# Four runs of unit-matrix products on TensorE, put into four of its pauses in a small vision tower

## The chip, the cores and the metric

The program runs on one core of a Trainium2 chip. The core's engines are TensorE (PE in the profile; PEld is its weight load, PEq or PEldq its instruction queue), VectorE (DVE), ScalarE (ACT), GpSimd (POOL) and SyncE (SP, which here only issues transfers). The metric is the device time of one execution in microseconds, the median of several runs.

## The reference

Inputs are 128 images. A token stage cuts each into 81 patches (a 14x14 convolution to 256 channels), attends over 3x3 windows and adds a class token, which gives h of 128 x 10 x 256. Four residual layers follow, each behind a layer norm:

```
h = tok(x, ...)                              # convolution, window attention, class token
h = h + attention0(layernorm(h), ...)        # 16 heads, 10 tokens, biases
h = h + moe(layernorm(h), ...)               # 8 experts, top 2, gelu, layer norm per expert
h = h + attention1(layernorm(h), ...)        # causal, scores clipped
h = h + lowrank(layernorm(h), ...)           # base matrix, shared and 6 routed low-rank pairs
```

The router picks two of eight experts for each of the 1280 tokens:

```
logits = x_flat @ router_w
gate_vals, gate_idx = jax.lax.top_k(logits, TOP_K)
h = jax.nn.gelu(jnp.einsum('nd,edf->enf', x_flat, w1) + b1[:, None, :], approximate=False)
out = jnp.einsum('enf,efd->end', h, w2) + b2[:, None, :]
```

## The kernel before

Each engine has its instructions written out by hand in one block, in the order in which it runs them, and semaphores tie the engines together. A matmul on fp32 operands shows as two MATMUL records (and two weight loads) in the profile; one on fp32r or bf16 operands, or a transpose, shows as one.

The stages in order of the span, with what TensorE does in them:

- **Convolution and window attention, from 13 to some 372 us.** TensorE waits for `consts_made` and `wc_made`, then for the first patch's operands (`x_lo_made`), and runs `LEAD` = 11 convolutions and then nine rounds.
- **Attention 0, to some 461 us.** Queries, keys and values, score sums with the unit matrix, output projection, and the router's logits.
- **Routing, to 482 us.** `pe_experts` begins with two products that count tokens per expert (lines 1682 and 1683, semaphore `route_summed`). VectorE (`dve_route`) works out each pair's place from them and writes one-hot matrices in four groups of five pairs (`row_hot_made`, line 1906). TensorE multiplies them (line 1689, `pairs_done`), VectorE turns the sums into tables of row numbers, GpSimd gathers the rows with indirect transfers (`rows_loaded`), and `turn_rows(0)` transposes the first 128 rows.
- **Experts, 482 to 681 us.** 27 blocks of 128 rows. For each, eight times `up` (line 1708, two 128x128 fp32 products) and `down` (line 1716, one 128x256 fp32 product), with gelu on ScalarE between them; `down` runs three behind `up`. Then gates are transposed, the experts' beta is added with eight-row products (line 1739), and two products with `z_w` (line 1744, semaphore `z_summed`) prepare the last layer.
- **Barrier, then the combine, attention 1 and the low-rank layer, 692 us to the end.** SyncE reads the experts' results back (`yl`), VectorE adds them to h and takes statistics (`dve_combine`), and attention 1 starts when its first tiles are normalized.

Between the experts and the combine stands a barrier over all five engines, `phase(eng, 2)`; the same call with 1 stands between the token stage and attention 0. Its two lines are

```
eng.drain().then_inc(sem("phase_ended"), 1)
eng.wait_ge(sem("phase_ended"), 5 * n)
```

so each engine goes on when all five have drained, and the drain is line 286 in the profile. On TensorE the order at that place is `pe_experts(pe)`, `phase(pe, 2)`, `pe_attention(pe, 1)`; on SyncE it is `phase(sp, 2)`, `sp_combine(sp)`.

The matmul destinations are PSUM banks 0 to 7; `bank(i, a, b)` is columns a to b of bank i. `ident` is the 128x128 fp32 unit matrix, one of the constants behind `consts_made`.

Of the kernel before, what the change touches and what calls it, by code (L numbers as in the profile page):

```python
# [22 lines left out]
P = 128  # L23
# [46 lines left out]
def vision_tower(nc, d, out):  # L70
    ctx = ExitStack()
    with ctx:
        def sb(name, shape, dt=F32, scope=None):
            return (scope or ctx).enter_context(nc.sbuf_tensor(name, shape, dt))
# [3 lines left out]
        def sem(name):  # L78
            if name not in sems:
                sems[name] = ctx.enter_context(nc.semaphore(name))  # L80
            return sems[name]
# [4 lines left out]
        def bank(i, a=0, b=C):  # L86
            return pair[i // 2][:, i % 2, a:b]
# [3 lines left out]
        ident = sb("ident", [P, P])  # L91
# [60 lines left out]
        rows = sb("rows", [P, len(ROWS) * C], F32, tok)  # L152
# [53 lines left out]
        count = sb("count", [P, P], F32, route)  # L206
# [94 lines left out]
        def turn(pe, dst, src):  # L301

            for c in range(CH):
                last = pe.transpose(dst[:, c * P:(c + 1) * P], src[:, c * P:(c + 1) * P], ident[:, :])  # L304
            return last

        class Chain:

# [105 lines left out]
        def conv(pe, i):  # L414
            k = i % RING_X
            if i >= 2:
                pe.wait_ge(sem("summed"), i - 1)
            pe.wait_ge(sem("x_lo_made"), 2 * i + 2)
            if i == NP:
                pe.wait_ge(sem("wc_made"), 7)  # L420
            for c in range(KF):
                a = [x[:, k, c * P:(c + 1) * P] for x in (x_hi, x_lo)]
                mm3(pe, bank(i % 2), a, (wc_hi[:, c, :], wc_lo[:, c, :]), c == 0, False)
            fourth, fifth = [x_hi[:, k, c * P:(c + 1) * P] for c in (KF, KF + 1)]
            if i < NP:
                last = mm3(pe, bank(i % 2), (fourth, fifth), (tail_hi, tail_lo), False, True)
            else:
                pe.matmul(bank(i % 2), fourth, wc_hi[:, KF, :], start=False, stop=False)
                last = pe.matmul(bank(i % 2), fifth, wc_hi[:, KF + 1, :], start=False, stop=True)  # L429
            last.then_inc(sem("conv_done"), 1)  # L430
# [58 lines left out]
        def turn_patch(pe, j):  # L489
            pe.wait_ge(sem("xn_made"), j + 1)  # L490
            if j >= 2:
                pe.wait_ge(sem("xg_lo_made"), j - 1)
            turn(pe, bank(2 + j % 2), xn[:, j % RING_XN, :]).then_inc(sem("xT_done"), 1)
# [1174 lines left out]
        def down_bank(s):  # L1668
            return bank(2 + 2 * (s % 2))

        def weights_of(s):
            r = s % RING
            return (w1raw[r], w2raw[r]) if r < 2 else (w1more[r - 2], w2more[r - 2])

        def loads_before(s):

            return s // RING

        def pe_experts(pe):
            pe.wait_ge(sem("route_consts"), ROUTE_CONSTS)  # L1680
            pe.wait_ge(sem("route_ready"), CH + 1)
            pe.matmul(bank(5, 0, E), before[:, :], rank[:, :, T - 1], start=True, stop=True)
            pe.matmul(bank(5, E, 2 * E), ones[:, :], rank[:, :, T - 1], start=True, stop=True)\
              .then_inc(sem("route_summed"), 1)

            for q in range(NPAIR):
                pe.wait_ge(sem("row_hot_made"), q // 5 + 1)
                pe.wait_ge(sem("col_hot_made"), 2)
                last = pe.matmul(bank(7, 0, 2 * NS), row_hot[:, q, :], col_hot[:, q, :], start=(q == 0), stop=(q == NPAIR - 1))
            last.then_inc(sem("pairs_done"), 1)  # L1690

            def turn_rows(s):
                pe.wait_ge(sem(f"rows_loaded{s % AHEAD}"), 16 * (s // AHEAD + 1))
                if s >= 2:
                    pe.wait_ge(sem("xT_made"), s - 1)
                elif s == 1:
                    pe.wait_ge(sem("tables_made"), 2)
                turn(pe, bank(6 + s % 2), xg[:, s % AHEAD, :]).then_inc(sem("rows_turned"), 1)

            def up(s, fc):  # L1700
                if fc == 0:
                    pe.wait_ge(sem("xT_made"), s + 1)
                    pe.wait_ge(sem(f"w_loaded{s % RING}"), 32 * (loads_before(s) + 1))
                g = s * FC + fc
                if g >= 2:
                    pe.wait_ge(sem("gelu_made"), g - 1)
                for c in range(CH):
                    last = pe.matmul(bank(fc % 2, 0, P), weights_of(s)[0][:, c * FF + fc * P:c * FF + (fc + 1) * P],  # L1708
                                     xT[:, s % 2, c * P:(c + 1) * P], start=(c == 0), stop=(c == CH - 1))
                last.then_inc(sem("up_done"), 1)  # L1710

            def down(s, fc):
                pe.wait_ge(sem("gelu_made"), s * FC + fc + 1)
                if fc == 0 and s >= 2:
                    pe.wait_ge(sem("res_made"), s - 1)
                last = pe.matmul(down_bank(s), hid[:, s % 2, fc, :], weights_of(s)[1][:, fc * C:(fc + 1) * C],  # L1716
                                 start=(fc == 0), stop=(fc == FC - 1))
                if fc == FC - 1:
                    last.then_inc(sem("down_done"), 1)

            turn_rows(0)
            for g in range(NS * FC + LAG):
                if g < NS * FC:
                    up(*divmod(g, FC))
                if g >= LAG:
                    down(*divmod(g - LAG, FC))
                if g < NS * FC and g % FC == 2 and g // FC + 1 < NS:
                    turn_rows(g // FC + 1)

            pe.wait_ge(sem("gates_made"), 1)  # L1730
            for i, (a, b) in enumerate(GROUPS):
                for t in range(a, b):
                    last = pe.transpose(bank((0, 1, 3)[i], (t - a) * P, (t - a + 1) * P)[0:E, :], gates[:, t, :], ident[:, :])
                last.then_inc(sem("g_turned"), 1)
            for t in range(T):
                pe.wait_ge(sem("gT_made"), t // 4 + 1)
                if t >= 4 and t % 2 == 0:
                    pe.wait_ge(sem("beta_added"), t // 2 - 1)
                last = pe.matmul(bank(6 + t // 2 % 2, t % 2 * C, (t % 2 + 1) * C), gT[:, t, :], beta[:, :], start=True, stop=True)
                if t % 2:  # L1740
                    last.then_inc(sem("beta_done"), 1)
            pe.wait_ge(sem("z_loaded"), 64)
            for c in range(CH):
                last = pe.matmul(bank(5, 0, ZW + C), ones[:, :], z_w[:, c, :], start=(c == 0), stop=(c == CH - 1))
            last.then_inc(sem("z_summed"), 1)

        def load_weights(sp, s, e):
            if s >= RING:
                sp.wait_ge(sem("down_done"), s - RING + 1)
            for dst, name in zip(weights_of(s), ("w1", "w2")):  # L1750
                sp.dma_start(dst[:, :], d[name][bass.ds(e * P, P), :]).then_inc(sem(f"w_loaded{s % RING}"), 16)
# [457 lines left out]
        @block.tensor  # L2209
        def _(pe):  # L2210
            pe.wait_ge(sem("consts_made"), 4)
            pe.wait_ge(sem("wc_made"), 4)
            for i in range(LEAD):
                if i == LEAD - 1:
                    turn_patch(pe, 0)
                conv(pe, i)
                if i == 1:
                    pe.wait_ge(sem("bias_columns"), CH)
                    mm_rows(pe, bank(4, 0, 2 * C), aggT, wkv_raw, 0, 2 * C).then_inc(sem("kvb_done"), 1)
                if i == 4:  # L2220
                    pe.wait_ge(sem("kvb_made"), 1)
                    turn(pe, bank(6), kvb[:, C:2 * C]).then_inc(sem("kvb_done"), 1)
                if i == LEAD - 1:
                    pe.wait_ge(sem("tok_w_loaded"), 128)
                    pe.wait_ge(sem("kvbT_made"), 1)
                    mm_rows(pe, bank(7), redT, w_proj, 0, C).then_inc(sem("kvb_done"), 1)
            pe.wait_ge(sem("wkv_lo_made"), CH)
            for n in range(NW):
                round_pe(pe, n)
            pe_end(pe)  # L2230
            phase(pe, 1)
            pe_attention(pe, 0)
            pe_experts(pe)
            phase(pe, 2)
            pe_attention(pe, 1)
            pe_lora(pe)
# [146 lines left out]
```

## Time and profile before

| | us |
|---|---|
| median of 3 runs | 802.9 (801.75 to 803.13) |
| the profiled execution, its own time | 801.32 |
| span of the profiled execution, first to last instruction | 799.3 |
| TensorE busy | 708.0 (89% of the span) |
| VectorE, ScalarE, GpSimd busy | 514.5, 378.1, 424.9 |
| TensorE's mean granted clock | 0.942 of 2.4 GHz |

The own time of the profiled execution is 2.0 us over its span, and 1.6 us under the median of the three. A busy TensorE says only that matmuls were under way, since they are pipelined and their ends are modelled. The granted clock of a stretch is 1.00 (2.4 GHz) or 0.50 (1.2 GHz); a mean between the two is a stretch that has both. The profile shows 1.00 from the start of the span until the first change of level that it recorded, whatever the engine ran at; in that stretch the spacing of the matmuls tells the level.

### The profile page before, as it was taken

The numbers are of one execution on the slowest core, as the hardware profiler recorded it, in microseconds if no ns is written. First come the engines' busy times: TensorE is split into PE (matmuls) and PEld (weight loads), VectorE is DVE, ScalarE is ACT, GpSimd is POOL, SyncE is SP. The second block draws the span as 40 slices with busy tenths as digits, with TensorE's granted clock in tenths as the row PEclk, the third lists the DMA queues.
The fourth block names the chain that finished last, engine by engine and source line by source line (L and its number), as shares of the span: only waits on it lengthen the run. The fifth ranks groups of instructions, "written<-read, shape, count | busy, mean of one in ns | idle before, by whom it ended". The sixth has DMA issues, their size and how long they took to land.

```text
span 799.3 us, 13085 instructions
## 1 busy us (share of the span) xinstructions
PE 708.0 (89%) x4247; PEld 606.5 (76%) x4247; DVE 514.5 (64%) x1230; ACT 378.1 (47%) x930; POOL 424.9 (53%) x360
## 2 busy tenths in 40 slices
PE   3879999999999999999829828999999999587797
PEld 2869998988889897654528727999999999344786
DVE  5758787878778777769989871322332223488957
ACT  4466666657666665533132323444444444056131
POOL 5765767677685771448959512333433332036640
PEclk9989999999999999999868967999999999689799
DMA  7952343333423220000020078899988982300001
GB/s 234 257 168 75 114 115 94 84 109 115 113 61 114 58 81 26 1 0 1 0 106 1 27 281 302 309 326 329 327 323 328 347 314 75 129 16 2 0 1 66
DMA packets 47065, 108.58 MB, mean 136 GB/s; under 512 B 5029, under 2 KB 24729, under 8 KB 39577
## 3 DMA queue, kind: packets, MB, share of 16 engines
q1 hardware_dynamic: 44408, 100.68, 37.7%
q0 software_dynamic: 2592, 7.10, 2.4%
q8 instruction: 35, 0.57, 0.3%
q14 instruction: 30, 0.24, 0.1%
HBM read 101.58 MB, written 6.17 MB: 135 GB/s over the span
## 4 chain that ended last, share of the span: by engine, by line
PE 74%; DVE 12%; DMA 4%; SPq 3%; POOL 3%; ACT 2%; issue 2%; DVEq 0%; ACTq 0%; POOLq 0%
PE banks L1708 12%; PE banks L1716 12%; PE banks L291 9%; PE banks L293 9%; PE banks L292 8%; PE banks L298 6%; PE banks L304 4%; PE banks L1316 3%; SPq L386 2%; DMA xraw<-in_x_rest 2%; PE banks L1363 1%; DVE banks L1490 1%; PE banks L1290 1%; DVE a_o L1581 1%; DVE a_prod L1203 1%
## 5 line engine op out<-in xcount | busy, mean ns | idle before, releaser
L408 POOL TENSOR_TENSOR x_lo<-xraw,x_hi 128x512 fp32r<-128x512 f32 x81 | 106.1, 1309 | 84.3 <-ACT x_hi L402 84.3
L1799 ACT ACTIVATE hid<-banks,b 128x128 f32<-128x128 f32 x216 | 79.3, 367 | 110.2 <-PE banks L1708 110.2
L291 PE MATMUL banks<-wc_hi,x_hi 128*128 128x256 f32 x324 | 97.3, 300 | 16.1 <-POOL x_hi L411 13.2
L1964 DVE TENSOR_TENSOR res<-banks,xb 128x256 f32<-128x256 f32 x27 | 11.5, 424 | 127.0 <-PE banks L1716 127.0
L293 PE MATMUL banks<-wc_hi,x_lo 128*128 128x256 f32 x324 | 92.2, 285 | 0.0
L292 PE MATMUL banks<-wc_lo,x_hi 128*128 128x256 f32 x324 | 92.1, 284 | 0.0
L291 PEld LDWEIGHTS banks<-wc_hi,x_hi 128*128 128x128 f32 x324 | 62.4, 193 | 18.5 <-issue 13.4
L442 DVE BATCH_NORM_STATS2 stats<-banks 128x6 f32<-128x256 f32 x81 | 34.6, 427 | 64.8 <-ACT pe_sb L436 64.2
L1837 POOL TENSOR_TENSOR y<-bve,mhalf 128x1 f32<-128x1 f32 x27 | 20.2, 748 | 105.2 <-DVE bve L1972 105.2
L1708 PEld LDWEIGHTS banks<-xT,w_raw 128*128 128x128 f32 x448 | 67.9, 196 | 5.8 <-ACT xT L1787 0.9
L436 ACT ACTIVATE pe_sb<-banks 128x256 f32<-128x256 f32 x81 | 31.0, 383 | 85.7 <-PE banks L429 76.9
L291 PE MATMUL banks<-wkv_hi,xg_hi 128*128 128x512 f32 x162 | 71.0, 438 | 0.2
L1708 PE MATMUL banks<-xT,w_raw 128*128 128x128 f32 x448 | 69.7, 280 | 0.5 <-ACT xT L1787 0.5
L402 ACT ACTIVATE x_hi<-xraw 128x768 fp32r<-128x768 f32 (+1 forms) x81 | 66.6, 828 | 7.1 <-DMA xraw<-in_x_rest 7.1
L1716 PE MATMUL banks<-w_raw,hid 128*128 128x256 f32 x224 | 67.1, 382 | 0.0
L1708 PEld LDWEIGHTS banks<-xT,w1more 128*128 128x128 f32 x416 | 61.9, 191 | 4.7
L293 PE MATMUL banks<-wkv_hi,xg_lo 128*128 128x512 f32 x162 | 64.3, 397 | 0.0
L292 PE MATMUL banks<-wkv_lo,xg_hi 128*128 128x512 f32 x162 | 64.0, 395 | 0.0
L292 PEld LDWEIGHTS banks<-wc_lo,x_hi 128*128 128x128 f32 x324 | 62.4, 192 | 1.8 <-issue 0.2
L340 POOL TENSOR_TENSOR rstd<-veps,mhalf 128x5 f32<-128x5 f32 (+5 forms) x31 | 32.9, 1061 | 57.5 <-DVE veps L358 37.4
L1708 PE MATMUL banks<-xT,w1more 128*128 128x128 f32 x416 | 63.2, 275 | 0.0
L1316 PE MATMUL banks<-a_w,a_xT 128*128 128x512 f32 (+1 forms) x160 | 62.5, 526 | 0.4 <-DVE w_raw L1503 0.3
(331 smaller groups left out, 1861.4 us busy)
## 6 DMA issues: line engine op xcount, KB each, us to landing
w_raw<-in_w SPq DMA_DIRECT2D x28, 1024.0 KB, 6.7
xraw<-in_x_main SPq DMA_DIRECT2D x27, 768.0 KB
w1more<-in_w SPq DMA_DIRECT2D x13, 1024.0 KB
w2more<-in_w SPq DMA_DIRECT2D x13, 1024.0 KB
xraw<-in_x_rest SPq DMA_DIRECT2D x48, 96.0 KB
xraw<-in_x_rest SPq DMA_DIRECT2D x27, 114.0 KB
yl<-y_rows SPq DMA_DIRECT2D x2, 1028.0 KB, 6.9
a_w<-in_qkv_w SPq DMA_DIRECT2D x2, 768.0 KB, 5.4
```

The lines of the kernel that those rows point to most:

```text
L291: pe.matmul(dst, a[0], b[0], start=start, stop=False)
L292: pe.matmul(dst, a[0], b[1], start=False, stop=False)
L293: return pe.matmul(dst, a[1], b[0], start=False, stop=stop)
L298: last = pe.matmul(dst, aT[:, c * P:(c + 1) * P], w[:, c, a:b], start=(c == 0), stop=(c == CH - 1))
L340: pool.tensor_tensor(rstd[i][:, a:b], veps[i][:, a:b], mhalf[:, a:b], ALU.pow).then_inc(sem("rstd_made"), 1)
L402: act.activation(x_hi[:, i % RING_X, 0:nc_used * P], xraw[:, k, 0:nc_used].rearrange("p c b -> p (c b)"), ACT.Copy)\
L408: pool.tensor_tensor(x_lo[:, i % RING_X, :], xraw[:, k, 0:KF].rearrange("p c b -> p (c b)"), x_hi[:, i % RING_X, 0:KF * P], ALU.subtract). ...
L442: dve.bn_stats(stats[0][:, k, :], bank(i % 2)).then_inc(sem("stats_made0"), 1)
L1316: last = pe.matmul(dst, a_xT[:, t % 2, c * P:(c + 1) * P], a_w[layer][:, c, a:b], start=(layer == 1 and c == 0), stop=(c == CH - 1))
L1708: last = pe.matmul(bank(fc % 2, 0, P), weights_of(s)[0][:, c * FF + fc * P:c * FF + (fc + 1) * P], xT[:, s % 2, c * P:(c + 1) * P], start= ...
L1716: last = pe.matmul(down_bank(s), hid[:, s % 2, fc, :], weights_of(s)[1][:, fc * C:(fc + 1) * C], start=(fc == 0), stop=(fc == FC - 1))
L1799: act.activation(hid[:, s % 2, fc, :], bank(fc % 2, 0, P), ACT.Gelu, bias=b1[:, bass.ds(e * FC + fc, 1)]).then_inc(sem("gelu_made"), 1)
```

## The change

A new helper multiplies the unit matrix by itself `count` times into a PSUM bank, each product on its own (start and stop set), with no wait and no semaphore. It is called in four places: ahead of the first convolution (30 products, once `consts_made` is there), after the two counting products and ahead of the one-hot products (16), after the one-hot products and ahead of `turn_rows(0)` (20), and at the end of `pe_experts`, after the two products with `z_w` (38). Nothing reads what they write. No other engine's instructions change.

```
+        IDLE = {"inputs": 30, "ranks": 16, "first rows": 20, "last rows": 38}
+
+        def keep_busy(pe, dst, count):
+
+            for i in range(count):
+                pe.matmul(dst, ident[:, :], ident[:, :], start=True, stop=True)
...
             pe.matmul(bank(5, E, 2 * E), ones[:, :], rank[:, :, T - 1], start=True, stop=True)\
               .then_inc(sem("route_summed"), 1)
+            keep_busy(pe, bank(0, 0, P), IDLE["ranks"])
 
             for q in range(NPAIR):
...
+            keep_busy(pe, bank(0, 0, P), IDLE["first rows"])
             turn_rows(0)
...
             last.then_inc(sem("z_summed"), 1)
+            keep_busy(pe, bank(0, 0, P), IDLE["last rows"])
...
             pe.wait_ge(sem("consts_made"), 4)
+            keep_busy(pe, bank(7, 0, P), IDLE["inputs"])
             pe.wait_ge(sem("wc_made"), 4)
```

On TensorE, at the end of the experts, the kernel before has these instructions (products with the gates `gT`, then with `z_w`, then the first transpose of attention 1, which waits for the barrier's `phase_ended`):

```order
L1739 MATMUL banks<-beta,gT 128x256 [waits beta_added,gT_made]
L1739 MATMUL banks<-beta,gT 128x256 [waits gT_made]
L1744 MATMUL banks<-z_w,ones 128x374 [waits z_loaded]
L1744 MATMUL banks<-z_w,ones 128x374
L304 MATMUL banks<-ident,a_xn 128x128 [waits a_xn_made,phase_ended]
```

In the changed kernel, at the same place (its line numbers are 7 to 9 higher, and line 312 is the helper's matmul):

```order
L1748 MATMUL banks<-beta,gT 128x256 [waits beta_added,gT_made]
L1748 MATMUL banks<-beta,gT 128x256 [waits gT_made]
L1753 MATMUL banks<-z_w,ones 128x374 [waits z_loaded]
L1753 MATMUL banks<-z_w,ones 128x374
L312 MATMUL banks<-ident 128x128 x38
L304 MATMUL banks<-ident,a_xn 128x128 [waits a_xn_made,phase_ended]
```

The 38 products stand ahead of the instruction that waits for the barrier, and in the code ahead of the barrier's drain.

On TensorE, around the routing, the changed kernel has these (`rank` and `before` are the counting products, `col_hot` and `row_hot` the one-hot matrices, `xg` the gathered rows):

```order
L1689 MATMUL banks<-rank,before 128x8 [waits route_ready,route_consts]
L1690 MATMUL banks<-rank,ones 128x8
L312 MATMUL banks<-ident 128x128 x16
L1697 MATMUL banks<-col_hot,row_hot 128x54 [waits col_hot_made,row_hot_made] x20
L312 MATMUL banks<-ident 128x128 x20
L304 MATMUL banks<-ident,xg 128x128 [waits rows_loaded0]
```

The kernel before has the same rows without the two of line 312. The products stand ahead of instructions that wait for VectorE and for a transfer.

## Rows read from the trace of the kernel before

**Rows 1.** The page: the engines' busy time; the chain that ended last by engine
```profile
PE 708.0 (89%) x4247; PEld 606.5 (76%) x4247; DVE 514.5 (64%) x1230; ACT 378.1 (47%) x930; POOL 424.9 (53%) x360
...
PE 74%; DVE 12%; DMA 4%; SPq 3%; POOL 3%; ACT 2%; issue 2%; DVEq 0%; ACTq 0%; POOLq 0%
```

**Rows 2.** The chain that ended last, 0 to 56 us
```profile
38.80 6.98 DMA xraw<-in_x_rest
...
49.43 2.08 PE banks L298 x4
```

**Rows 3.** All engines in order of time, 450 to 500 us
```profile
463.88 0.58 PE L1683 MATMUL banks<-rank,ones 128*128 128x8 f32 x2
...
470.04 3.02 DVE L1906 TENSOR_TENSOR row_hot<-count_b,row_f 128x640 bf16<-128x640 bf16 x4
...
473.83 0.18 DVE L1921 TENSOR_SCALAR who<-banks 128x27 f32<-128x27 f32 x1 [0.77 <-PE banks L1689]
...
482.03 0.69 PE L304 MATMUL banks<-ident,xg 128*128 128x128 f32 x2 [8.23 <-DMA xg<-x_rows,src]
```

**Rows 4.** Stretches: length, busy of PE, PEld, DVE, ACT, POOL, granted clock, DMA
```profile
44.90:47.30 2.40, 0.00 (x0) 0.00 (x0) 0.35 (x2) 1.50 (x4) 2.40 (x3) 1.00 0.31 98
47.30:49.40 2.10, 0.00 (x0) 0.00 (x0) 2.06 (x6) 2.10 (x6) 2.10 (x5) 0.50 0.31 55
49.40:54.10 4.70, 4.67 (x12) 3.72 (x13) 4.60 (x9) 2.13 (x5) 1.75 (x4) 0.50 0.76 236
...
463.70:471.00 7.30, 0.84 (x5) 0.75 (x6) 6.08 (x22) 2.50 (x5) 0.00 (x0) 0.50 0.58 210
...
482.00:487.60 5.60, 5.10 (x21) 4.66 (x22) 0.43 (x1) 1.61 (x5) 0.95 (x1) 0.50 0.93 299
487.60:500.00 12.40, 12.40 (x87) 11.63 (x86) 2.01 (x6) 5.55 (x16) 2.70 (x3) 1.00 0.75 290
...
685.60:691.20 5.60, 5.54 (x11) 2.76 (x9) 1.82 (x3) 0.00 (x0) 0.00 (x0) 0.50 0.07 24
692.30:701.60 9.30, 0.00 (x0) 0.00 (x0) 5.09 (x16) 0.66 (x2) 1.82 (x2) 0.50 0.75 283
701.60:706.00 4.40, 4.28 (x8) 2.09 (x9) 4.11 (x15) 0.81 (x2) 0.30 (x1) 0.50 0.02 4
706.10:714.40 8.30, 7.29 (x27) 4.20 (x25) 6.64 (x21) 6.62 (x16) 3.20 (x3) 1.00 0.00 0
```

**Rows 5.** PE in order of time, in the middle of the experts
```profile
672.99 0.60 PE L1716 MATMUL banks<-w_raw,hid 128*128 128x256 f32 x2
673.43 0.61 PE L1708 MATMUL banks<-xT,w1more 128*128 128x128 f32 x4
673.87 0.60 PE L1716 MATMUL banks<-w_raw,hid 128*128 128x256 f32 x2
```

**Rows 6.** The chain that ended last, 678 to 724 us; start, length (us), what
```profile
688.35 2.81 PE banks L1744 x4
...
691.80 0.49 DVEq L286
692.31 3.80 DMA yl<-y_rows
...
714.46 2.82 PE banks L1316 x8
```

**Rows 7.** All instructions of line 286, the barrier's drain, each engine's queue
```profile
L286 PEldq DRAIN  x2: 3648/4306/4963, 400.7 to 686.2; - x2
```

**Rows 8.** PE's weight loads grouped by line, 500 to 670 us
```profile
L1708 PEld LDWEIGHTS banks<-xT,w_raw 128*128 128x128 f32 x374 | 55.6, 191 | 4.2
```

**Rows 9.** PE in order of time, one of the first convolution's pauses
```profile
31.44 0.39 PE L291 MATMUL banks<-wc_hi,x_hi 128*128 128x256 f32 x1 [1.73 <-DVE red_sum L449]
```

**Rows 10.** All engines in order of time, 0 to 20 us
```profile
2.50 0.14 POOL L2188 IOTA iota<- 128x8 f32 x1
...
13.20 0.29 PEld L291 LDWEIGHTS banks<-wc_hi,x_hi 128*128 128x128 f32 x1 [13.20 <-issue]
```

More of the change, by code:

```diff
@@ L305, in turn, with keep_busy @@
             return last
+        IDLE = {"inputs": 30, "ranks": 16, "first rows": 20, "last rows": 38}
+        def keep_busy(pe, dst, count):
+            for i in range(count):
+                pe.matmul(dst, ident[:, :], ident[:, :], start=True, stop=True)
         class Chain:
@@ L1684, in pe_experts @@
               .then_inc(sem("route_summed"), 1)
+            keep_busy(pe, bank(0, 0, P), IDLE["ranks"])
             for q in range(NPAIR):
@@ L1719, in down @@
                     last.then_inc(sem("down_done"), 1)
+            keep_busy(pe, bank(0, 0, P), IDLE["first rows"])
             turn_rows(0)
@@ L1745, in pe_experts @@
             last.then_inc(sem("z_summed"), 1)
+            keep_busy(pe, bank(0, 0, P), IDLE["last rows"])
         def load_weights(sp, s, e):
@@ L2211, in _ @@
             pe.wait_ge(sem("consts_made"), 4)
+            keep_busy(pe, bank(7, 0, P), IDLE["inputs"])
             pe.wait_ge(sem("wc_made"), 4)
```

## The prediction

> **What bounds the kernel now.** First the page: TensorE is busy 89% of the span and carries 74% of the chain that ended last [rows 1]. So what matters is where TensorE is not on that chain, and where it is on it at half clock. Second, the chain around each of the four places. Ahead of the first convolution it runs through GpSimd and the image transfers, and TensorE first appears on it at 49.43 [rows 2]. Around the routing it runs through VectorE and the gather that lands at 482.03 [rows 3]. From there to 691 the experts keep TensorE busy without a break [rows 4, 5]. After that comes the barrier: the products with z_w end at 691.16 (688.35 + 2.81), VectorE finishes z_w and drains until 692.29, and at 692.31 the transfer of the experts' results begins; TensorE is not on the chain again until 714.46 [rows 6]. Third, the drains: the barrier's second drain on TensorE starts at 686.2 and lasts 4.963, so it ends at 691.16, with the last matmul. TensorE's queue had run ahead, and the drain held until the matmuls were through [rows 7]. Fourth, the granted clock by stretch: 0.50 from 463.7 to 487.6 and from 685.6 to 706.1; also from 47.3 to 54.1, which no edit touches [rows 4].
>
> **The price of one product.** In the experts four records of 128 columns and two of 256 repeat every 0.88 us (672.99 to 673.87) [rows 5]: eight units of 128 columns, 0.110 each. A unit-matrix product is two records of 128 columns, so 0.22 us at full clock. At the 0.50 level twice that, 0.44; the z_w products at that level give a bound of 0.48 (2.81 for four records of 374 columns, times 128/374, times two) [rows 6].
>
> How long until the clock rises: nearly unbroken work at 0.50 lasted 4.7 us (49.4 to 54.1), 4.4 (701.6 to 706.0) and, with breaks, 5.6 (482.0 to 487.6) before the level was 1.00 [rows 4]. I use 4.4 to 5.6.
>
> Weight loads take 191 ns each [rows 8], longer than the 110 ns between records, but they overlap one another and the matmuls, so I cost them at nothing. The Trainium skill, TensorE: Matmul & The Clock Gate, Part 3, The mechanism, says that a weight load overlaps matmuls in flight only when it goes to another row group; all of these use all rows, so by it loads and matmuls would alternate, and 38 products would take 76 x (0.191 + 0.110) = 22.9 us in place of 8.4, and the change 14.5 us more. The experts' rows contradict it: loads to the same rows recur there and cost no time.
>
> **Last rows: 38 products ahead of the barrier.** They start at 691.16, at 0.50. The dense work began at 688.35, so the clock should rise 4.4 to 5.6 us after that, at 692.75 to 693.95: 1.6 to 2.8 us at 0.44 (3.6 to 6.4 products), the rest at 0.22 (7.6 to 7.0 us). That is 9.2 to 9.8 us; end at 700.4 to 700.9. If the clock were up at once: 8.4, end at 699.5. If it never rose: 16.7, end at 707.9.
>
> TensorE's drain comes behind them, so the barrier opens at 700.4 to 700.9 in place of 692.3. Queued behind it on every engine is the whole rest: SyncE's transfer, VectorE's combine, GpSimd's and ScalarE's part of attention 1. VectorE's z_w edit is released by `z_summed` before the products and ends as now. Nothing can run in the 8 us, so they go onto the end whole: **+8.2** (7.2 to 8.6).
>
> Does it give anything back? Now the clock is at 0.50 until 706.0 [rows 4]. After the change TensorE's first transposes come as long after the barrier as now, some 9.4 us (692.3 to 701.7) after its last product. The clock fell 2.4 us after the convolution's last matmul at 44.9, at 47.3 [rows 4], and held through a pause of 1.7 [rows 9]; 9 us should drop it. And were it up, the chain from 692 to 714 is transfer, VectorE and GpSimd [rows 6], so a faster start of TensorE there is hidden: **0**.
>
> **First rows: 20 products ahead of the first transposes.** TensorE is free at 473.8 and the rows land at 482.03 [rows 3]. The products take 4.4 us (full clock) to 8.8 (never up; 0.6 late, which is the loss at most). If the clock is at 0.50 when they start, it rises after 4.4 to 5.6 us, with 10 to 13 products done; the rest take 2.2 to 1.6 us; they end at 480.4 to 481.0, 1.0 to 1.6 us before the rows, a pause that the clock has survived. If it is up already, they end at 478.2 and leave 3.8 us, longer than the pause after which it fell. What an early clock is worth: 5.1 us of TensorE work from 482.0 to 487.6 at 0.50 [rows 4], so 2.5 at most, on the chain. I take half, **-0.8 to -1.2**, since either start can hold.
>
> **Ranks: 16 products ahead of the one-hot products.** They start at 464.46 (463.88 + 0.58) [rows 3] and last 3.5 to 7.0 us, so until 468 to 471.5. The first one-hot group could come 0.6 late, but the chain hangs on the last, whose matrices are done at 473.06 (470.04 + 3.02) and whose sums VectorE has 0.77 later [rows 3]; with TensorE free, nothing is lost. With the clock up, half of that 0.77 less a fixed part is saved: **-0.3**, bounds 0 and -0.4. The two edits work against each other, since a clock raised early by this one is what lets the next one's products end too early. Both together: **-1.0**, 0 to -2.8.
>
> **Inputs: 30 products ahead of the first convolution.** They last 6.6 us (full) to 13.2 (never up) from about 2.7, the end of the constants [rows 10], and with a rise after 4.4 to 5.6 us some 8.8 to 9.4: done by 12.1, ahead of the first convolution at 13.2 [rows 10]. That one then runs at 2.4 GHz, but TensorE is on the chain there nowhere before 49.43: GpSimd's subtractions release SyncE's transfers, and the last of those lands at 45.8 (38.80 + 6.98) [rows 2]. TensorE waits for the images anyway. Were they late by 2.7 (never up), the pauses of the first convolutions would take it. **0**.
>
> **Sum.** +8.2 - 1.0 = +7.2. The profiled execution took 801.3 and lies 1.6 under the median of the runs, 802.9; on the median I forecast **810.1**.
>
> **Rivals.**
>
> 1. *The barrier doesn't wait for the products.* TensorE's drain would count only what is issued. Then +8.2 falls away and -1.0 (0 to -2.8) is left: 801.9, at best 800.1. What decides is whether SyncE's transfer starts at 692.3 or at 700.5. Against it: both drains of this queue lasted microseconds, and the last ended with the last matmul [rows 7]. Chance 0.05; of that 0.03 is within 0.2%, 0.02 faster.
> 2. *The unit matrix doesn't raise the clock,* since its operands are almost all zeros. Then 38 products take 16.7 us, the barrier opens at 707.9, and the first rows come 0.6 late: +16.2, 819.1. For it: no row of dense products with `ident` on both sides exists. Against it: matmul records are matmul records in the rows that rose. Chance 0.05.
> 3. *Weight loads alternate with matmuls*, by the mechanism priced above from the load's 191 ns: the barrier opens at 714.1, +21.8, near 824. The experts' spacing speaks against it. Chance 0.02.
>
> **How the numbers follow.** The forecast has 0.88. Its terms run from +4.4 (7.2 - 2.8, the clock up at once and the whole gain at the experts) to +9.2 (8.6 + 0.6): 807.3 to 812.1. The runs of before scatter by 1.4, so the range is 806.8 to 812.5; it leaves out the rivals, 0.12, and some of the forecast's edges. Within 0.2% (1.6 us, about what a measurement of this kernel can tell from no change): rival 1's 0.03. Faster: 0.02. Slower: 0.95.
>
> **What would show it right or wrong.** After: TensorE's second drain should be about 9 us longer, end at 700 to 701, and the transfer of yl start right behind it; from there every row to the end is shifted by 8. The 76 records of the last place should be 0.11 apart once the clock is up. TensorE's clock at the first transposes of attention 1 should be 0.50 again. The stretch from the gather's landing to the third block of the experts should be 0 to 2.5 us shorter. The start to 49.4 should not move. A transfer of yl at 692 would make the forecast wrong; so would a clock at 0.50 through all 38 products, or an early clock in attention 1 that shortens the stretch from yl to the end by microseconds.

## The result, and the profile after

The changed kernel takes 814.67 us (median of 4 runs, 812.89 to 815.97) against 802.56 for the kernel before in the same comparison (4 runs, 801.75 to 803.13). The ratio is 1.0145, with a 95% interval of 1.0129 to 1.0161: 11.6 us slower (10.4 to 12.9). The forecast of +7.2 had the sign, and its range ended at 812.5, too low. The profiled execution of the changed kernel took 812.89 (span 810.8), 11.6 over that of before, and is the fastest of its four.

The page of the changed kernel, against [rows 1]: TensorE is busy for 30.4 us more, with 208 records more, and its share of the chain that ended last is smaller, not larger.

```profile
PE 738.4 (91%) x4455; PEld 635.6 (78%) x4455; DVE 516.0 (64%) x1230; ACT 377.9 (47%) x930; POOL 424.9 (52%) x360
...
PE 72%; DVE 13%; DMA 4%; POOL 3%; ACT 3%; issue 2%; PEld 1%; SPq 1%; PEldq 0%; DVEq 0%; ACTq 0%; POOLq 0%
```

The barrier first. The instructions of line 286 in the changed kernel, against [rows 7]:

```profile
L286 PEldq DRAIN  x2: 2173/2910/3648, 402.6 to 700.3; - x2
```

TensorE's second drain now starts at 700.3 and lasts 2.173, so it ends at 702.5, in place of 691.16. The chain that ended last shows what stands ahead of it, in the place of [rows 6] (start, length, what):

```profile
692.87 7.63 PEld banks L312 x59
700.49 2.01 PEldq L286
702.52 3.89 DMA yl<-y_rows
...
724.77 1.53 PE banks L1323 x3
```

The chain now runs through the weight loads of the new products and the drain behind them, and the transfer of `yl` follows within 0.03 us. It starts at 702.52, 10.21 later than in [rows 6]. The products with z_w began 1.86 later than there (690.21 against 688.35), so the 38 products cost 8.35 at the barrier. TensorE in order of time shows the same, and how attention 1 then begins:

```profile
690.21 2.86 PE L1753 MATMUL banks<-z_w,ones 128*128 128x374 f32 x4
692.87 9.61 PE L312 MATMUL banks<-ident 128*128 128x128 f32 x76
711.98 1.09 PE L304 MATMUL banks<-ident,a_xn 128*128 128x128 f32 x4 [9.51 <-ACT a_xn L375]
```

First the transposes at the gather's landing, in TensorE's order of time. Then stretches of the changed kernel, with the columns of [rows 4]: around the gather, the last products, and the first transposes of attention 1.

```profile
484.47 0.44 PE L304 MATMUL banks<-ident,xg 128*128 128x128 f32 x2 [2.81 <-DMA xg<-x_rows,src]
```

```profile
480.00:484.40 4.40, 1.66 (x15) 1.47 (x14) 0.00 (x0) 0.00 (x0) 3.49 (x4) 1.00 1.03 352
484.40:486.60 2.20, 1.60 (x10) 1.17 (x10) 0.42 (x1) 0.77 (x3) 0.28 (x1) 1.00 0.96 359
486.60:490.00 3.40, 3.39 (x14) 3.21 (x15) 0.00 (x0) 1.08 (x3) 0.00 (x0) 0.51 1.00 342
490.00:500.00 10.00, 10.00 (x70) 9.38 (x70) 2.01 (x6) 4.59 (x13) 1.41 (x2) 1.00 0.70 271
692.90:694.90 2.00, 2.00 (x11) 2.00 (x10) 1.00 (x2) 0.00 (x0) 0.00 (x0) 0.51 0.00 0
694.90:702.40 7.50, 7.50 (x68) 7.38 (x67) 0.00 (x0) 0.00 (x0) 0.00 (x0) 1.00 0.00 0
...
711.90:715.30 3.40, 3.28 (x7) 1.73 (x8) 3.21 (x10) 0.81 (x2) 0.30 (x1) 0.50 0.00 0
```

The reader is to see three things. Once the clock is up, 68 records take 7.5 us, 0.110 each, as forecast. At the first transposes of attention 1 it is at 0.50 again, as forecast. And after the gather's landing at 484.47 it is up for 2 us, falls for 3.4 and is up again: the early clock that the first rows were to bring was there and did not last.

At the start, TensorE in order of time shows the products of the inputs and the first convolution (before, the first record came at 13.23, and records stood 0.21 apart up to 16.36):

```profile
2.70 9.85 PE L312 MATMUL banks<-ident 128*128 128x128 f32 x60 [2.70 <-POOL iota L2198]
13.58 0.35 PE L291 MATMUL banks<-wc_hi,x_hi 128*128 128x256 f32 x1 [1.03 <-POOL x_hi L418]
13.78 0.28 PE L292 MATMUL banks<-wc_lo,x_hi 128*128 128x256 f32 x1
13.89 0.28 PE L293 MATMUL banks<-wc_hi,x_lo 128*128 128x256 f32 x1
```

They are done in time (2.70 + 9.85 = 12.55), and from the second record on the first convolution's records stand 0.11 to 0.12 apart. In this execution that led to neither gain nor loss: the convolution at 56.28 on the chain of before stands at 56.31.

To split the 11.5 us by place I set VectorE's instructions, which are the same 1230 in both profiled executions, against each other and read how much later each one begins:

```
time in before   later by
 56              0.0
342              1.8
482              2.4     (the gather has landed)
688              1.9     (ahead of the barrier)
696              10.3    (first instruction of the combine)
753              11.2
760 to the end   11.5
```

The 1.8 at 342 is a fall of the clock to 0.50 from 339.9 to 343.3. The profiles of runs 8, 10 and 11 below have it too, of which runs 8 and 10 have no product ahead of it; the profiles of the other runs do not. So I take it for scatter of single executions, and count by medians from here on. The median of the changed kernel is 1.8 above its profiled execution, so this split is that of one execution and not of the median: it holds 8.4 at the barrier, 1.8 at this fall, and nothing from the inputs.

### The profile page after: what moved, and what is told of

It reads as the page before. It is cut to its first block, busy times and chain, and to the rows that moved or that the text cites. A ratio compares the mean times of both kernels' runs of the same rounds, so it can differ in the third digit from the quotient of the medians.

```text
span 810.8 us, 13501 instructions
## 1 busy us (share of the span) xinstructions
PE 738.4 (91%) x4455; PEld 635.6 (78%) x4455; DVE 516.0 (64%) x1230; ACT 377.9 (47%) x930; POOL 424.9 (52%) x360
## 4 chain that ended last, share of the span: by engine, by line
PE 72%; DVE 13%; DMA 4%; POOL 3%; ACT 3%; issue 2%; PEld 1%; SPq 1%; PEldq 0%; DVEq 0%; ACTq 0%; POOLq 0%
PE banks L1716 12%; PE banks L1724 12%; PE banks L291 9%; PE banks L293 8%; PE banks L292 8%; PE banks L298 6%; PE banks L304 4%; PE banks L1323 3%; DMA xraw<-in_x_rest 2%; PE banks L1370 2%; DVE banks L1497 1%; PE banks L1297 1%; DVE a_o L1588 1%; DVE a_prod L1210 1%; PE banks L1353 1%
## 5 line engine op out<-in xcount | busy, mean ns | idle before, releaser
L1974 DVE TENSOR_TENSOR res<-banks,xb 128x256 f32<-128x256 f32 x27 | 11.5, 425 | 126.6 <-PE banks L1724 126.6
```

## The experiments

Twelve kernels were timed in five rounds each against the kernel before on the same chip. All compute the whole reference. Diffs stand against the changed kernel. The last column is the ratio's difference from 1, in us.

| run | products | median (low to high, runs) | before | ratio (95%) | us |
|---|---|---|---|---|---|
| 1 | last 38 | 811.39 (810.56 to 811.80, 4) | 802.24 | 1.0113 (1.0098 to 1.0127) | +9.1 |
| 2 | inputs, ranks, first | 806.55 (804.17 to 808.54, 6) | 802.24 | 1.0048 (1.0032 to 1.0064) | +3.9 |
| 3 | all, last 38 behind the barrier | 807.58 (802.17 to 809.87, 12) | 802.24 | 1.0055 (1.0038 to 1.0073) | +4.4 |
| 4 | inputs | 805.41 (801.84 to 807.50, 9) | 802.24 | 1.0030 (1.0014 to 1.0046) | +2.4 |
| 5 | ranks, first | 802.25 (800.86 to 804.33, 12) | 802.10 | 1.0000 (0.9988 to 1.0013) | 0.0 |
| 6 | inputs; scalings on ScalarE | 801.23 (799.88 to 802.83, 12) | 802.10 | 0.9987 (0.9977 to 0.9998) | -1.0 |
| 7 | none; scalings on ScalarE | 801.62 (800.34 to 802.85, 12) | 802.10 | 0.9987 (0.9974 to 1.0000) | -1.0 |
| 8 | last 19 | 806.60 (805.28 to 808.71, 6) | 802.10 | 1.0054 (1.0035 to 1.0074) | +4.3 |
| 9 | ranks, first 28 | 801.75 (798.17 to 804.06, 12) | 803.08 | 0.9993 (0.9979 to 1.0008) | -0.6 |
| 10 | first 28 | 800.74 (798.39 to 801.71, 12) | 803.08 | 0.9974 (0.9963 to 0.9985) | -2.1 |
| 11 | inputs, 10 in place of 30 | 802.55 (801.20 to 805.08, 12) | 803.08 | 0.9998 (0.9988 to 1.0009) | -0.2 |
| 12 | ranks, first 28; scalings on ScalarE | 798.28 (797.60 to 799.88, 6) | 803.08 | 0.9951 (0.9936 to 0.9966) | -3.9 |

### The last rows: runs 1, 8 and 3

**Run 1** keeps only the 38 products ahead of the barrier.

```
-            keep_busy(pe, bank(0, 0, P), IDLE["ranks"])
-            keep_busy(pe, bank(0, 0, P), IDLE["first rows"])
-            keep_busy(pe, bank(7, 0, P), IDLE["inputs"])
```

> Only the 38 products at the end of the experts are left; the other three places are as before. Theory A (the barrier waits for them, and what the changed kernel lost beyond that came from where the clock happened to fall): +8.5 to +10 us against the kernel before; in the trace TensorE's drain ends some 9.6 us after the z_w products and the yl transfer starts 10 us later than before, while all up to the z_w products lies within 0.5 us of before unless the clock falls elsewhere by itself. Theory B (the products ahead of the convolution, at the ranks or at the first rows cost the other 3 us, by moving where the clock falls in attention 0): +8.2 to +8.6 and no slower, and attention 0 without a fall at 340 us. Theory C (the 38 products also cost attention 1 and the low-rank layer, behind the barrier): +11 to +12.

It cost 9.1 us (7.9 to 10.2). Line 286 in its profile:

```profile
L286 PEldq DRAIN  x2: 2173/2910/3648, 400.8 to 698.3; - x2
```

The drain ends at 700.5, where the prediction had put it (700.4 to 700.9), and VectorE's first instruction of the combine comes 8.20 later than before. Behind the barrier another 1.1 is lost: the last of VectorE's instructions come 9.3 later. The stretch of attention 1 at the lower clock, of before and then of run 1, is where it goes:

```profile
736.80:750.40 13.60, 6.70 (x23) 5.75 (x23) 12.58 (x14) 2.70 (x7) 7.97 (x5) 0.50 0.00 1
```

```profile
747.20:760.90 13.70, 9.01 (x32) 7.97 (x33) 12.75 (x12) 2.46 (x7) 6.00 (x6) 0.50 0.00 1
```

It ends 10.5 later while the work around it is 8.2 later, so more of TensorE's work falls into it: 32 records and 9.01 us in place of 23 and 6.70. The changed kernel shows the same (749.5 to 763.1). Only single profiles show this, and it does not hang on the products alone: in run 4, which has none at the barrier, VectorE goes from 5.2 late to 5.7 late over this stretch, and in run 8, which has 19, from 5.8 to 5.6. No run tested it, and run 1's interval holds 8.2 without it.

**Run 8** halves the count.

```
-        IDLE = {"inputs": 30, "ranks": 16, "first rows": 20, "last rows": 38}
+        IDLE = {"inputs": 30, "ranks": 16, "first rows": 20, "last rows": 19}
-            keep_busy(pe, bank(0, 0, P), IDLE["ranks"])
-            keep_busy(pe, bank(0, 0, P), IDLE["first rows"])
-            keep_busy(pe, bank(7, 0, P), IDLE["inputs"])
```

> Only the products at the end of the experts, 19 of them in place of the 38 of run 1. If the barrier waits for them, 19 x 0.22 us less than run 1's +9.1: +4.5 to +5.5. If the cost hung on the clock or on the tail behind the barrier and not on their length: +8 to +9, or near 0.

It cost 4.3 us (2.8 to 5.9), 4.8 less than run 1 and a little under what was expected; 19 products at 0.22 are 4.2. Its chain that ended last:

```profile
692.88 3.13 PEld banks L312 x21
696.01 2.01 PEldq L286
698.04 3.86 DMA yl<-y_rows
```

The drain and the transfer follow the last product here too. So the cost goes with the length of the products, and not with their being there.

**Run 3** keeps all four calls, but puts the 38 products behind the barrier.

```
             last.then_inc(sem("z_summed"), 1)
-            keep_busy(pe, bank(0, 0, P), IDLE["last rows"])
...
             pe_experts(pe)
             phase(pe, 2)
+            keep_busy(pe, bank(0, 0, P), IDLE["last rows"])
             pe_attention(pe, 1)
```

> All four places, but the 38 products stand behind the barrier and ahead of attention 1's first wait. Theory A: the yl transfer starts at the old distance from VectorE's drain, 8 to 10 us of the loss are gone, so -2.5 to +1 against the kernel before; TensorE's clock is at 1.00 in attention 1's first products, which the chain there (transfer and VectorE) hides. Theory B: +2 to +4. Theory C: the tail behind the barrier is longer than before by 1 us or more whenever the 38 products are there.

It cost 4.4, where theory A allowed +1 at most, beside the 3.9 of run 2, which has no such products at all; what is left is that of the other places. Its chain that ended last:

```profile
697.21 0.55 DVE z_w L1995
697.76 0.49 DVEq L286
698.27 3.89 DMA yl<-y_rows
```

As in [rows 6], VectorE's drain is the last to end and the transfer follows it; TensorE's drain is off the chain. So it is the place ahead of the drain that costs 8 us, and nothing else about these products. It also shows that they buy nothing: in run 3 TensorE goes from them to the transposes without a pause, and run 3 is no faster than run 2.

### The three other places: runs 2, 4 and 5

**Run 2** leaves out the 38 products, **run 4** keeps the inputs alone, **run 5** the ranks and the first rows.

```
run 2
-            keep_busy(pe, bank(0, 0, P), IDLE["last rows"])
run 4
-            keep_busy(pe, bank(0, 0, P), IDLE["ranks"])
-            keep_busy(pe, bank(0, 0, P), IDLE["first rows"])
-            keep_busy(pe, bank(0, 0, P), IDLE["last rows"])
run 5
-            keep_busy(pe, bank(0, 0, P), IDLE["last rows"])
-            keep_busy(pe, bank(7, 0, P), IDLE["inputs"])
```

> The 38 products at the end of the experts are gone, the other three places stay. Theory A: between -2 and +1 us against the kernel before, with the barrier's transfer right behind VectorE's drain again. Theory B: +2 to +4 us, with a fall of the clock in attention 0 near 340 us. Theory C: -1 to 0.

> Only the 30 products ahead of the first convolution. Theory A: within 1 us of the kernel before; the first convolution runs with 0.12 us between matmuls, and nothing behind 49 us moves. Theory B: +1.5 to +3 us, as a fall of the clock in attention 0 appears that was not there before. Theory C: 0.

> Only the 16 products at the ranks and the 20 at the first rows. The two-place theory (the loss is the barrier plus a delay of VectorE at the start, and these two give what the prediction said): -0.3 to -2.8 us against the kernel before, with the start to 460 us as before. The rival that these two places lose by themselves (run 2 was 1.1 us slower than run 4, which lacks them): +0.5 to +1.5.

By the prediction run 2 was to be faster than before by about 1, and it is slower by 3.9. Run 4 shows that the inputs, costed at nothing, cost 2.4 (1.1 to 3.7). Run 5 shows no gain from the other two places (-1.0 to +1.0), where -1.0 was forecast. With run 1 the parts come to 9.1 + 2.4 + 0.0 = 11.5, against 11.6 measured for the whole. That they meet so closely is partly luck: run 2 has the inputs and the two other places together, and 9.1 + 3.9 is 13.0.

Theory B had the right size for run 4, but not the right place. Its profile has no fall of the clock near 340; VectorE is 3.9 late by 56 us already, of 5.7 in the whole of that execution (807.00, well above run 4's median). Where that comes from stands in its chain that ended last, 0 to 64 us:

```profile
18.98 0.59 DVE kvb L2307
19.57 6.91 DVE wkv_raw L2309 x2
26.48 0.34 DVE stats L449
26.82 0.33 DVE red_sum L456
27.20 0.58 PE banks L291
```

In [rows 2] this stretch belonged to the images. Here it belongs to two instructions of VectorE that scale the weights `wkv_raw`, 6.91 us long. VectorE's sums of the convolution (`red_sum`) stand behind them in its order, and TensorE waits 4.78 us for those. The two scalings in before, in run 4 and in run 2 (least, median and greatest duration in ns, first and last start):

```profile
L2301 DVE TENSOR_SCALAR wkv_raw<-wkv_raw,vecs x2: 794/1156/1519, 20.9 to 21.6; 128x512 f32<-128x512 f32 x2
```

```profile
L2309 DVE TENSOR_SCALAR wkv_raw<-wkv_raw,vecs x2: 3529/3536/3544, 19.5 to 22.9; 128x512 f32<-128x512 f32 x2
```

```profile
L2311 DVE TENSOR_SCALAR wkv_raw<-wkv_raw,vecs x2: 473/3850/7227, 19.4 to 26.6; 128x512 f32<-128x512 f32 x2
```

The same instruction takes 0.47 us at best, in run 2 once GpSimd's chain is over, and 7.23 at worst. With the first convolution at full clock VectorE comes to it 1.4 to 1.5 us earlier (19.4 and 19.5, not 20.9). GpSimd in run 4 at that time, in order of time:

```profile
19.36 0.46 POOL L418 TENSOR_TENSOR x_hi<-xraw,x_hi 76x128 fp32r<-76x128 f32 x1
19.79 1.28 POOL L415 TENSOR_TENSOR x_lo<-xraw,x_hi 128x512 fp32r<-128x512 f32 x1
21.04 0.46 POOL L418 TENSOR_TENSOR x_hi<-xraw,x_hi 76x128 fp32r<-76x128 f32 x1
21.46 1.27 POOL L415 TENSOR_TENSOR x_lo<-xraw,x_hi 128x512 fp32r<-128x512 f32 x1
22.71 0.63 POOL L418 TENSOR_TENSOR x_hi<-xraw,x_hi 76x128 fp32r<-76x128 f32 x1
...
26.16 0.63 POOL L418 TENSOR_TENSOR x_hi<-xraw,x_hi 76x128 fp32r<-76x128 f32 x1
```

GpSimd subtracts without a break until 26.8, and the second scaling ends at 26.5, inside the last of these subtractions. The Trainium skill, SBUF — State Buffer, Who interferes with whom, says that VectorE's `tensor_scalar` can use a pair of ports that it shares with GpSimd, that whoever issues first holds the pair for its instruction, and that the other is blocked. The trace agrees that VectorE stands still beside a busy GpSimd; which ports the scalings used, no row shows. A wait for one GpSimd instruction would make 0.47 + 1.28 = 1.75 us at most. 3.53 and 7.23 were measured, so here VectorE waited through several.

GpSimd's chain alone is not what sets run 4 apart. In before GpSimd is in the same chain, also until 26.8, and the scalings took 0.79 and 1.52 beside it. What differs is how many of its instructions go by before VectorE has its turn. GpSimd in before:

```profile
21.38 1.47 POOL L408 TENSOR_TENSOR x_lo<-xraw,x_hi 128x512 fp32r<-128x512 f32 x1
22.80 0.65 POOL L411 TENSOR_TENSOR x_hi<-xraw,x_hi 76x128 fp32r<-76x128 f32 x1
```

Both are some 0.2 longer than their kind (1.27 and 0.46), and the two scalings end inside them, at 21.7 and 23.1. In run 4 the subtractions at 22.71 and 26.16 are longer by 0.17, and the scalings end inside these, at 23.0 and 26.5. In run 2 none is longer, and the first scaling ends at 26.65 (19.42 + 7.23), after the chain's last subtraction (26.4).

### Is it the meeting with GpSimd: runs 6, 7 and 11

**Run 6** has the inputs' 30 products and moves the two scalings to ScalarE; **run 7** is its control, with the scalings moved and no product at all.

```
-            for c in range(CH):
-                dve.tensor_scalar(wkv_raw[:, c, :], wkv_raw[:, c, :], vecs[:, LAKV + c:LAKV + c + 1], None, ALU.mult)\
-                   .then_inc(sem("wkv_scaled"), 1)
...
+                    act.wait_ge(sem("kvb_made"), 1)
+                    for c in range(CH):
+                        act.activation(wkv_raw[:, c, :], wkv_raw[:, c, :], ACT.Identity, scale=vecs[:, LAKV + c:LAKV + c + 1])\
+                           .then_inc(sem("wkv_scaled"), 1)
```

> The 30 products ahead of the convolution, and the two scalings of wkv_raw, which took VectorE 7.0 us in run 4 beside GpSimd's chain of subtractions and 2.3 us in the kernel before, moved from VectorE to ScalarE, just ahead of the copies that use them. Theory D (VectorE's two scalings are held up by GpSimd when the first convolution is early): the 3.2 us of run 4 are gone but for what ScalarE's two more instructions cost, which run 7 shows; so within 1 us of run 7. Rival E (the products ahead of the convolution cost by themselves, through the clock's later falls or the transfers): 2 to 4 us above run 7.

> The control: the kernel before, none of the products, with the two scalings moved from VectorE to ScalarE. Theory D: -1 to +1.5 us against the kernel before, since VectorE's 2.3 us there had little behind them. Rival E: the same.

Both ratios are 0.9987: without the scalings on VectorE the inputs' products cost nothing. They bring nothing either, which is what the prediction said of the clock there. In run 6 ScalarE does the two scalings like this, while GpSimd is in its chain:

```profile
L2263 ACT ACTIVATE wkv_raw<-wkv_raw,vecs x2: 714/714/715, 25.3 to 25.9; 128x512 f32<-128x512 f32 x2
```

**Run 11** leaves the scalings on VectorE and cuts the 30 products to 10, which are over long before the first convolution.

```
-        IDLE = {"inputs": 30, "ranks": 16, "first rows": 20, "last rows": 38}
+        IDLE = {"inputs": 10, "ranks": 16, "first rows": 20, "last rows": 38}
-            keep_busy(pe, bank(0, 0, P), IDLE["ranks"])
-            keep_busy(pe, bank(0, 0, P), IDLE["first rows"])
-            keep_busy(pe, bank(0, 0, P), IDLE["last rows"])
```

> Only the products ahead of the first convolution, 10 in place of the 30 of run 4. They end by some 7 us, six before the first convolution, so its matmuls should be at half clock again, VectorE come to its two scalings as late as in the kernel before, and those take some 2.3 us in place of 7.0. Theory D (what costs is the early convolution, which brings VectorE's scalings under GpSimd's chain): 0 within 0.7 us of the kernel before. A rival, that the products themselves cost at the start (their reads of SBUF or their instructions beside the transfers): +1 or more.

It cost nothing (-0.2, -1.0 to +0.7). Its first convolution ran at the lower clock, and the scalings began at 21.4:

```profile
13.20:15.20 2.00, 1.48 (x7) 1.51 (x8) 2.00 (x2) 0.00 (x0) 2.00 (x4) 0.50 0.56 180
```

```profile
L2309 DVE TENSOR_SCALAR wkv_raw<-wkv_raw,vecs x2: 1906/2056/2205, 21.4 to 23.5; 128x512 f32<-128x512 f32 x2
```

So in these runs the products cost time only when they make the first convolution faster, and only while VectorE has the scalings to do. Still, how long the scalings take is not a matter of the start alone. In the changed kernel's profiled execution they began at 19.8 and took 3.8, which left no delay at 56. In run 11's they began at 21.4, later than in before, and took 4.1 in place of 2.3, and VectorE is 1.2 late at 56; that execution is the slowest of run 11's twelve (805.08). That fits a spread from 801.84 to 807.50 in run 4.

### What the first rows could be worth: runs 9, 10 and 12

In run 5 the 20 products are over too early. Its stretches around the gather (columns of [rows 4]):

```profile
477.50:480.30 2.80, 2.80 (x26) 2.67 (x24) 0.00 (x0) 0.00 (x0) 2.19 (x3) 1.00 1.02 432
480.40:482.30 1.90, 0.00 (x0) 0.00 (x0) 0.00 (x0) 0.00 (x0) 1.46 (x2) 1.00 1.10 392
482.30:484.20 1.90, 1.35 (x10) 1.11 (x10) 0.47 (x1) 0.48 (x2) 0.94 (x1) 1.00 0.80 235
484.40:487.60 3.20, 3.18 (x13) 2.97 (x13) 0.00 (x0) 1.17 (x4) 0.00 (x0) 0.50 0.95 305
487.70:494.00 6.30, 6.30 (x45) 5.89 (x44) 0.00 (x0) 2.84 (x8) 0.00 (x0) 1.00 0.72 299
```

TensorE pauses for 2.0 us (480.4 to 482.4), and the clock holds through the pause and through the first transposes. Then it falls at 484.4, for 3.2 us of solid work, and is up again at 487.7, where before it rose at 487.6 [rows 4]. Little of the gain is left: VectorE's instructions are 0.35 late at the landing and 0.17 early in the first block, which makes 0.5 us in this execution; the medians show none.

**Run 9** has 28 products for the first rows in place of 20, with the ranks' 16; **run 10** has the 28 alone.

```
-        IDLE = {"inputs": 30, "ranks": 16, "first rows": 20, "last rows": 38}
+        IDLE = {"inputs": 30, "ranks": 16, "first rows": 28, "last rows": 38}
-            keep_busy(pe, bank(0, 0, P), IDLE["last rows"])
-            keep_busy(pe, bank(7, 0, P), IDLE["inputs"])
run 10 too
-            keep_busy(pe, bank(0, 0, P), IDLE["ranks"])
```

> Run 5 with 28 products in place of 20 at the first rows (16 at the ranks as there). In run 5 the 20 ended 2.0 us before the gathered rows landed, the clock was at 1.00 at the landing and fell 1.9 us later for 3.4 us, so that the experts reached full clock when they did before. Theory F (that pause took the gain back): with the products lasting until the landing the clock stays at 1.00, and -1 to -2.5 us against the kernel before. Rival G (the clock falls in the thin start of the experts anyway, or the experts' start isn't bound by TensorE): 0 within 0.5 us.

> The 28 products at the first rows alone. They start at the 0.50 level, so they take some 8 to 8.6 us and end with the landing or 0.5 us behind it. Theory F: -0.5 to -2 us. Rival G: 0 to +0.5.

TensorE's first transposes in run 9, and its stretches:

```profile
483.07 0.44 PE L304 MATMUL banks<-ident,xg 128*128 128x128 f32 x2 [0.49 <-DMA xg<-x_rows,src]
```

```profile
478.40:482.40 4.00, 4.00 (x37) 3.99 (x36) 0.00 (x0) 0.00 (x0) 3.09 (x4) 1.00 1.04 425
482.40:486.00 3.60, 2.56 (x19) 1.96 (x18) 0.42 (x1) 1.16 (x4) 1.11 (x2) 1.00 1.07 304
486.00:494.00 8.00, 8.00 (x58) 7.51 (x57) 0.69 (x2) 3.67 (x11) 0.00 (x0) 1.00 0.85 321
```

The products last until 482.6, the rows land at 483.07, and the clock does not fall again: 58 records in the 8 us from 486. By VectorE's instructions run 9 goes from 1.0 late at the landing to 1.0 early in the first block, a gain of 2.0 where run 5 has 0.5. Run 10's profile gains 2.0 there too (from 3.0 late to 1.0 late), and by its median it is 2.1 faster than before (1.2 to 3.0), though its products begin at the lower clock. Run 9's median shows 0.6, under the 1 to 2.5 expected, and its interval (-1.7 to +0.6) takes in zero and overlaps that of run 5; its twelve times lie between 798.17 and 804.06. So that lasting until the landing keeps the clock up is shown by the profiles, and a gain by the median of run 10 alone. Whether the ranks' products take something back in run 9, or it is scatter, stays open.

The profiles of runs 9 and 10 hold a second gain that was not forecast. Between 685 and 692 they win another 1.4 each: the clock falls 5.4 and 5.5 us after the eight-row products of the experts' beta begin (at 681.16, to 686.6, in run 9), and 3.5 after them in before (682.15, to 685.6 [rows 4]). Run 5 has no such gain. Whether it belongs to the 28 products or to where the clock happened to fall, no run shows.

**Run 12** joins what helped: the ranks' 16, 28 for the first rows, the scalings on ScalarE, nothing ahead of the first convolution and nothing ahead of the barrier. Its diff is that of run 9 and the move of the scalings from run 7.

> The products at the ranks (16) and at the first rows (28), none ahead of the barrier and none ahead of the convolution, and the scalings on ScalarE as in run 7. If theories D and F hold, the gains of runs 7 and 9 add: -1.5 to -3.5 us against the kernel before. If F falls: as run 7, -0.5 to -1.

It takes 798.28, 3.9 us less than before (2.7 to 5.1) and the fastest of all. The gains of runs 9 and 7 make 1.6, those of runs 10 and 7 3.1; against run 7 its profile shows the same two places as run 9's, 1.7 at the landing and 1.5 at the end of the experts.

## Why the prediction was wrong

- **"Last rows: +8.2" was right in its mechanism.** The barrier waits for the products; at the barrier itself 8.35 in the changed kernel and 8.20 in run 1 lie within the 7.2 to 8.6. Run 1's median, 9.1 (7.9 to 10.2), is 0.5 over that. Rival 1 falls with the drain and the transfer, and with runs 3 and 8. That attention 1 gains nothing was right too. Two profiles lose some 1.1 us more behind the barrier; run 4 loses 0.5 there without any such product, so this is not shown to be the products' doing.
- **"Inputs: 0" is the step that failed,** by 2.4 us (run 4). Its reason was that TensorE is nowhere on the chain before 49.43 and waits for the images anyway. That is true, and bounds only the gain. I did not ask what a faster first convolution sets off: VectorE comes to its two scalings 1.4 us earlier, with more of GpSimd's chain of subtractions still ahead, stands still for up to 7 us beside it, and TensorE then waits 4.8 us for the sums queued behind them (run 4). With the scalings off VectorE the same products cost nothing (run 6 against run 7). Why VectorE waits so long in some executions and not in others stays open. The only loss I had considered there was products that end late.
- **"Together -1.0" for the ranks and the first rows was not there either:** 0.0 (-1.0 to +1.0) in run 5, at the edge of the 0 to -2.8 given. The products ended 1.0 to 1.6 us ahead of the rows in the prediction and 2.0 in run 5. The pause itself was survived, as [rows 9] had let me expect; what I took from that, that the clock then stays, was wrong. The idea of the gain was sound: with products up to the landing, run 10 gains 2.1, within the 0 to -2.8, and its profile 2.0 at the landing; half of 5.1 us, 2.5, had been put as the most.
- **The price of a product was right:** 0.110 a record in the changed kernel, so 0.22 for each product. The unit matrix raises the clock (rival 2 falls), and loads to the same rows cost no time (rival 3 falls).
- **The sum:** forecast 8.2 + 0 - 1.0 = 7.2; measured by single runs 9.1 + 2.4 + 0.0 = 11.5. Of the 4.3 between them 2.4 are the inputs', 1.0 the gain that did not come, and 0.9 the last rows'. The range was too narrow because it gave the inputs no loss at all; the 0.6 on the side of a loss was that of products at the first rows that end late.

## What to carry to other kernels

In this kernel TensorE's drain ended only with the last matmul that was queued ahead of it, and every other engine waited for that drain. So filler ahead of the barrier was paid in full, and behind the drain it cost nothing that the runs show. Filler that is to hold a clock up has to last until the real work arrives: 20 products that ended 2.0 us early gained nothing that the medians show, and 28 that lasted until the landing, alone, gained 2.1 us (run 10). And when a step off the critical path is made faster, a cost of zero is not the floor: look up what it releases, and what that runs into.

## What the runs showed of the hardware

- One instruction of VectorE, a 128x512 `tensor_scalar` in fp32, took 7.23 us beside GpSimd instructions of 0.45 to 1.29 us, and 0.47 us right after, once these were over (both in run 2). Why it gets its turn soon in one execution and late in another, with GpSimd equally busy, is not settled.
- The clock can fall after a pause is over: in run 5 it held through 2.0 us of pause and 2.0 of transposes and first products, and then gave 0.50 for 3.2 us to an engine that was busy for 3.18 of them.
- Products of a matrix that is almost all zeros raise the clock too: from 0.51 to 1.00 within 2.0 us of their start in the changed kernel, 4.7 us after the products with z_w began.
